# Pairs of token tiles taken from a host-transposed copy of x and normalised by GpSimd, instead of normalised by ScalarE and transposed by TensorE

## The reference

```
x = x + layernorm(attention(layernorm(x)))     # 16 heads of 16, causal softmax, Wq, Wk, Wv, Wo of 256 x 256
x = x + layernorm(moe(layernorm(x)))           # 8 experts, top 2 of a softmax router, 256 -> 2 x 512 -> 256
layernorm(x) = (x - mean(x)) / sqrt(var(x) + 1e-5)     # over the 256 features, no weights
```

## Time and profile before

| | |
|---|---|
| median of 3 runs | 1974.83 us (1972.89 to 1975.65) |
| profiled execution, its own time | 1972.61 us |
| its span, first to last instruction | 1970.9 us |
| TensorE matmul busy | 1843.2 us (94%) |
| VectorE / ScalarE / GpSimd busy | 1541.8 / 1310.9 / 865.1 us |
| mean granted TensorE clock | 0.979 |

### The profile page before, as it was taken

The page is one execution under the profiler, slowest core; times in us unless marked ns, Lnnn a source line. Parts: engine busy times, 40 slices in busy tenths (PEclk is TensorE's granted clock), DMA queues, the critical chain, the costliest instruction groups (busy, mean ns, idle before and its releaser), DMA issues.

```text
span 1970.9 us, 75491 instructions
## 1 busy us (share of the span) xinstructions
PE 1843.2 (94%) x26766; PEld 1280.2 (65%) x26767; DVE 1541.8 (78%) x5221; ACT 1310.9 (67%) x3291; POOL 865.1 (44%) x1247
## 2 busy tenths in 40 slices
PE   6899999999999999999999899999999999999980
PEld 3245555555545555455444369999999999999970
DVE  3888888888888888888888658778777777777767
ACT  5177788888888888888787766554445445554437
POOL 4333343445545555555454744544333333333336
PEclk9799999999999999999999999999999999999995
DMA  7744657475655656465557569889899999998848
GB/s 203 219 120 131 196 171 213 150 208 183 184 172 170 189 154 203 137 192 158 167 163 234 169 206 279 240 250 265 252 260 264 257 264 261 264 262 245 239 119 342
DMA packets 255062, 411.72 MB, mean 209 GB/s; under 512 B 34480, under 2 KB 191920, under 8 KB 247600
## 3 DMA queue, kind: packets, MB, share of 16 engines
q1 hardware_dynamic: 217856, 363.46, 57.7%
q0 software_dynamic: 27120, 35.40, 10.2%
q10 hardware_dynamic: 9792, 8.93, 1.5%
HBM read 284.83 MB, written 122.28 MB: 207 GB/s over the span
## 4 chain that ended last, share of the span: by engine, by line
PE 84%; DVE 6%; ACT 4%; issue 3%; DMA 2%; SPq 1%; POOL 0%; DVEq 0%; ACTq 0%; POOLq 0%
PE ps_s L1544 18%; PE ps_s L1375 12%; PE ps_o L1428 12%; PE ps_e L1375 11%; PE ps_w L1375 11%; PE ps_e L1544 6%; PE ps_e L1561 6%; PE ps_o L1561 6%; DVE cmax L792 2%; ACT space L1275 2%; PE ps_e L1554 1%; ACT arena L1167 1%; DVE space L128 1%; PE ps_w L1504 1%; PE ps_w L1441 1%
## 5 line engine op out<-in xcount | busy, mean ns | idle before, releaser
L1167 ACT ACTIVATE arena<-ps_e 128x512 f32<-128x512 f32 (+3 forms) x1536 | 675.5, 498 | 191.8 <-PE ps_e L1375 179.0
L789 DVE CUSTOM_DVE_ANT_0 arena<-ps_s,c 128x384 bf16<-128x384 f32 (+3 forms) x1024 | 461.7, 485 | 117.2 <-PE ps_s L1375 113.5
L1375 PE MATMUL ps_e<-arena 98*32 98x512 bf16 (+3 forms) x6144 | 505.2, 327 | 28.2 <-ACT arena L1167 27.3
L1375 PE MATMUL ps_s<-arena 96*32 96x512 bf16 (+3 forms) x6144 | 509.0, 333 | 10.7 <-DVE rmax L789 3.7
L792 DVE TENSOR_REDUCE cmax<-ps_s 128x1 f32<-128x512 f32 x512 | 322.5, 680 | 28.9 <-PE ps_s L1375 28.1
L1375 PEld LDWEIGHTS ps_s<-arena 96*32 96x32 bf16 x6144 | 177.8, 96 | 211.7 <-DVE rmax L789 80.8
L1428 PE MATMUL ps_o<-arena 128*32 128x512 f32 (+3 forms) x3072 | 296.3, 486 | 6.1 <-ACT ot L1181 3.2
L1375 PEld LDWEIGHTS ps_e<-arena 98*32 98x32 bf16 x6144 | 177.7, 96 | 178.8 <-issue 82.0
L669 POOL DMA_INDIRECT acc<-blank,place_now x135 | 213.3, 1580 | 140.6 <-POOL place_now L662 66.1
L1544 PE MATMUL ps_s<-arena 128*128 128x128 f32 x2192 | 268.5, 276 | 0.8 <-ACT arena L1314 0.7
L1544 PEld LDWEIGHTS ps_s<-arena 128*128 128x128 f32 x2192 | 261.4, 192 | 8.4 <-issue 3.2
(11 more groups left out here) (182 smaller groups left out, 2714.5 us busy)
## 6 DMA issues: line engine op xcount, KB each, us to landing
arena<-in_gate_up SPq DMA_DIRECT2D x91, 1024.0 KB, 6.0
arena<-qk_parts SPq DMA_DIRECT2D x384, 128.0 KB
c_h<-in_gate_up SPq DMA_DIRECT2D x44, 1024.0 KB
qk_parts<-space SPq DMA_DIRECT2D x120, 192.0 KB, 4.4
d_xin<-xs SPq DMA_DIRECT2D x136, 130.5 KB, 3.4
arena<-v_aug SPq DMA_DIRECT2D x32, 512.0 KB, 5.0
o_t<-ot SPq DMA_DIRECT2D x64, 256.0 KB
v_aug<-space SPq DMA_DIRECT2D x28, 512.0 KB, 5.6
```

The lines of the kernel that those rows point to most:

```text
L789: dve.tensor_tensor_reduce(summed[:, m % RJ, 0:w], ps_s[:, m % RS, 0:w], after[:, HALF - w:HALF], 1.0, LOWEST, ALU.add, ALU.max, rmax[:, p ...
L1167: act.activation(pw[:, at % RP, begin:end], ps_e[:, n % RE, 0:w], ACT.Exp, scale=SCALE).then_inc(e_done, 1)
L1375: last = pe.matmul(out[at:at + QUAD], lhsT[:, at:at + QUAD], rhs, start=start, stop=stop)
```

## The change

For the pairs from 6 to 31 (26 of 32) the host hands in a second copy of x, transposed (`x_turned`, features by tokens). SyncE loads its 256 columns of the pair straight into `xn_t`. TensorE turns the pair's four columns of statistics (1/std and shift of two tiles, `a_norm`, 128 x 4) into four rows by one matmul with the identity; ScalarE copies the 4 x 128 result out; SyncE writes it to memory as four rows of 512 bytes, and loads it back broadcast to all partitions (`norm_rows`, in the place of `xn`). GpSimd then multiplies and adds, two instructions of 128 x 512. The two normalise instructions, the four transposes and the copy to `xn_t` go away for these pairs. The q and k steps of these pairs stand one slot earlier (`Q_AT`); `route` moves from s = 1 to s = 3 of its slot for all pairs. The load of x waits for the statistics alone. Some semaphores are merged, and one 128 x 1 memset of GpSimd goes away. The last fill with ones now waits for `xn_t` of pair 6.

```diff
+    Q_AT = [start if a < FIRST_EVEN else start - 1 for a, start in enumerate(A_AT)]
+    NORM_AT = [start - (12 if a == FIRST_EVEN else 13) for a, start in enumerate(A_AT)]
...
+        norm_rows = space[:, 2560:3072].rearrange("p (z t) -> p z t", z=2)
...
+        turned_v = x_turned.rearrange("(k p) (a t) -> a p k t", p=P, t=WIDE)
+        norms_v = norms.rearrange("a z (c p) -> a (z c) p", p=P)
...
 SyncE
-                        sp.wait_ge(a_xn, a - 1 if a < EARLY else a + 1)
+                        if a < FIRST_EVEN:
+                            sp.wait_ge(a_xn, a - 1 if a < EARLY else a + 1)
+                        else:
+                            sp.wait_ge(a_st, a + 1)
                         sp.dma_start(ax[:, a % 2], x_v[a + 2]).then_inc(ax_in[a % 2], 16)
+                for a in due(A_AT, -12, g):
+                    if a >= FIRST_EVEN:
+                        sp.wait_ge(norms_sb, a - FIRST_EVEN + 1)
+                        sp.dma_start(norms_v[a], norm_row[:]).then_inc(norms_out, 16)
+                for a in due(A_AT, -10, g):
+                    if a >= FIRST_EVEN:
+                        u = a % 2
+                        sp.wait_ge(a_v, a - 1)
+                        sp.wait_ge(a_xt, a)
+                        sp.dma_start(xn_t[:, u], turned_v[a]).then_inc(turned_in, 16)
+                        sp.wait_ge(norms_out, (a - FIRST_EVEN) * 16 + 16)
+                        if a == FIRST_EVEN:
+                            sp.wait_ge(a_tps, FIRST_EVEN)
+                        sp.dma_start(norm_rows, norms[a:a + 1].broadcast_to([P, 2, WIDE])).then_inc(turned_in, 16)
...
 GpSimd
-            pool.memset(pad[:, 0:1], 0.0).then_inc(carried, 1)
-            pool.wait_ge(carried, 1)
...
-                for u, (at, done_by, n) in enumerate(((BEGIN - 2, a_p3, 2 * EARLY + 2), (BEGIN + 6, a_p3, 2 * EARLY + 4), (BEGIN + 9, a_p3, 2 * EARLY + 4))):
+                for u, (at, done_by, n) in enumerate(((BEGIN - 2, a_p3, 2 * EARLY + 2), (BEGIN + 6, a_p3, 2 * EARLY + 4), (BEGIN + 9, a_xt, FIRST_EVEN + 1))):
...
+                for a in due(A_AT, -7, g):
+                    if a >= FIRST_EVEN:
+                        u, mine = a % 2, xn_t[:, a % 2]
+                        pool.wait_ge(turned_in, (a - FIRST_EVEN) * 32 + 32)
+                        pool.tensor_tensor(mine, mine, norm_rows[:, 0:1].broadcast_to([P, KT, WIDE]), ALU.mult).then_inc(a_scaled, 1)
+                        pool.wait_ge(a_scaled, a - FIRST_EVEN + 1)
+                        pool.tensor_tensor(mine, mine, norm_rows[:, 1:2].broadcast_to([P, KT, WIDE]), ALU.add).then_inc(a_xt, 1)
...
-                for a in due(A_AT, 6, g):
+                for a in due(Q_AT, 6, g):
                     third(a, 1)
-                for a in due(A_AT, 3, g):
+                for a in due(Q_AT, 3, g):
                     third(a, 0)
...
 VectorE
-                        for a in due(A_AT, 2, g):
+                        for a in due(Q_AT, 2, g):
                             remainder(a, 0)
-                        for a in due(A_AT, 4, g):
+                        for a in due(Q_AT, 4, g):
                             remainder(a, 1)
...
 ScalarE
                     if s == 1:
+                        for a in due(NORM_AT, 0, g):
+                            if a >= FIRST_EVEN:
+                                act.wait_ge(norms_ps, a - FIRST_EVEN + 1)
+                                if a > FIRST_EVEN:
+                                    act.wait_ge(norms_out, (a - FIRST_EVEN) * 16)
+                                act.activation(norm_row[:], ps_w[0:4, 0:P], ACT.Copy).then_inc(norms_sb, 1)
...
                     if s == 2:
-                        for a in due(A_AT, 0, g):
+                        for a in due(A_AT[0:FIRST_EVEN], 0, g):
                             act.wait_ge(a_tps, a + 1)
...
-                        for a in due(A_AT, 2, g):
+                        for a in due(Q_AT, 2, g):
                             first_part(a, 0)
...
-                        for a in pairs_due(-2, -10, g):
+                        for a in due(A_AT[0:FIRST_EVEN], -2, g):
...
 TensorE
+            def turn_norms(a):
+
+                bank_free()
+                used.append((norms_sb, a - FIRST_EVEN + 1))
+                pe.wait_ge(a_shifted, a + 1)
+                pe.matmul(ps_w[0:4, 0:P], a_norm[:, a % 2].rearrange("p z c -> p (z c)"), consts["ident"],
+                          start=True, stop=True).then_inc(norms_ps, 1)
...
                     if s == 0:
...
+                        for a in due(NORM_AT, 0, g):
+                            if a >= FIRST_EVEN:
+                                turn_norms(a)
-                        for a in due(A_AT, 4, g):
+                        for a in due(Q_AT, 4, g):
                             q_or_k(a, 1, (1,))
                     if s == 1:
-                        for a in due(A_AT, 0, g):
+                        for a in due(A_AT[0:FIRST_EVEN], 0, g):
                             turn_over(a)
-                        for a in due(A_AT, 1, g):
+                        for a in due(Q_AT, 1, g):
                             q_or_k(a, 0, (0, 1))
...
-                        for r in rows_due(16, 17, 17, g):
-                            route(r, 0)
-                            route(r, 1)
...
+                    if s == 3:
                         for r in rows_due(16, 17, 17, g):
                             route(r, 0)
                             route(r, 1)
```

More of the change, by code:

```diff
@@ L153, in combine_stage, with attention_layer @@
     return on_sync, on_gpsimd, on_scalar, on_vector
-def attention_layer(nc, x, wq_t, wk_t, wv_t, wo_t, router_t, router_bias, qk_parts, v_aug, o_t, rden, x1, xs, acc, consts, ident_b, after,
+def attention_layer(nc, x, x_turned, wq_t, wk_t, wv_t, wo_t, router_t, router_bias, qk_parts, v_aug, o_t, rden, norms, x1, xs, acc, consts, ident_b, after,
                     constants_in, kept, expert_weights, w_dn_in, biases_in, gate_up, arena, x1_all, x1_in, load_x1, out):
@@ L271, in attention_layer @@
         a_minus = sb("a_minus", [P, 2, 2])
-        a_rstd = sb("a_rstd", [P, 2, 2])
-        a_shift = sb("a_shift", [P, 2, 2])
+        a_norm = sb("a_norm", [P, 2, 2, 2])
+        a_rstd, a_shift = a_norm[:, :, 0], a_norm[:, :, 1]
+        norm_row = sb("norm_row", [4, P])
         w_o = sb("w_o", [P, KT, D])
@@ L352, in attention_layer @@
         loads, v_loads = ([sem(f"{n}{s}") for s in range(SETS)] for n in ("loads", "v_loads"))
-        rows_in, ones, carried = sem("rows_in"), sem("b_ones"), sem("b_carried")
+        rows_in, ones = sem("rows_in"), sem("b_ones")
         s_scores, s_cmax, s_rmax, s_mhi, s_mlo = (sem("s_" + n) for n in ("scores", "cmax", "rmax", "mhi", "mlo"))
@@ L362, in attention_layer @@
         ax_early = sem("ax_early")
-        a_st, a_agg, a_varred, a_negated, a_rooted, a_shifted = (sem("a_" + n) for n in ("st", "agg", "var", "neg", "root", "shift"))
+        a_st, a_agg, a_moved, a_rooted, a_shifted = (sem("a_" + n) for n in ("st", "agg", "moved", "root", "shift"))
         a_xn, a_tps, a_xt, a_qk, a_p1, a_r1, a_p2, a_p3, a_v, a_vout = (sem("a_" + n) for n in (
@@ L367, in attention_layer @@
         v_out = [sem(f"v_out{u}") for u in range(2)]
+        turned_in, norms_out, a_scaled, norms_ps, norms_sb = (sem(n) for n in ("turned_in", "norms_out", "a_scaled", "norms_ps", "norms_sb"))
         c_weights_in = sem("c_weights_in")
@@ L371, in attention_layer @@
         den_in, rd_out, rd_loads, cx_in = ([sem(f"{n}{u}") for u in range(2)] for n in ("den_in", "rd_out", "rd_loads", "cx_in"))
-        c_den, c_on, c_w, c_raw, c_st, c_agg, c_varred, c_negated, c_rooted, c_shifted = (sem("c_" + n) for n in (
-            "den", "on", "w", "raw", "st", "agg", "var", "neg", "root", "shift"))
+        c_den, c_on, c_w, c_raw, c_st, c_agg, c_moved, c_rooted, c_shifted = (sem("c_" + n) for n in (
+            "den", "on", "w", "raw", "st", "agg", "moved", "root", "shift"))
         c_yn, c_x1, c_hn, c_tps, c_ht, c_r, c_lg, c_top, c_ix = (sem("c_" + n) for n in (
@@ L379, in attention_layer @@
         scattered = [sem(f"scattered{u}") for u in range(2)]
-        base_set, sel_set, zero_at_ready, zeros_out, chain, tables = (sem("g_" + n) for n in ("base_set", "sel_set", "zero_at", "zeros", "chain", "tables"))
+        base_set, zero_at_ready, zeros_out, chain, tables = (sem("g_" + n) for n in ("base_set", "zero_at", "zeros", "chain", "tables"))
         x_in = [sem(f"d_x_in{s}") for s in range(RX)]
@@ L770, in _ @@
             for sel in sels.values():
-                dve.memset(sel[:], 0.0).then_inc(sel_set, 1)
+                dve.memset(sel[:], 0.0).then_inc(base_set, 1)
             for e in range(E):
@@ L1602, in _ @@
                             turn_rows(r)
+                        for n in groups_due(NEVER, 23, g, 1):
+                            rank(n)
+                    if s == 2:
+                        for a in due(Q_AT, 3, g):
```

(7 more changed lines are left out.)

40 lines of the change are left out of this document (19 added, 21 removed).

## The result

The changed kernel takes 2021.82 us (median of 4 runs, 2019.36 to 2025.31) beside 1974.34 us (median of 4, 1972.89 to 1975.65): a ratio of 1.0242, 95% interval 1.0224 to 1.0260. It is 2.4% slower. The profiled execution took 2025.31 us, its span is 2023.6, so that between the two profiled executions there are 52.7 us.

A forecast was written before the change was run, and what follows sets the result against it. TensorE, busy 97%, was taken as the bound. Slots 8 to 0 (+10), slot 7 (+21) and the start (+12) made +43 us on the profiled 1972.6; as a median 2018, less 2 for slack: 2016 us, range 2000 to 2028.

The forecast's parts named there:

- the 2 us taken off for slack: Whole sum: 2018 lowered to 2016 us, since waits that follow each other share slack not visible in one quad.
- The start: Pair 6's loads queue behind SyncE's stores, delaying GpSimd and quad 0's `max_rows`: +12 us, bounds 0 to 16.
- Slots 8 to 0: Transposes and an exponential wait go, new waits come in slots 10 and 0: +0.43 us a quad, 10 us together.
- the old stall: Slot 11, quads 0 to 23: TensorE's wait for an exponential behind `first_part` and the normalise, 1.09 us by starts of matmuls.
- Slot 7: The turning matmul costs 0.24 us and waits for GpSimd's statistics: 1.05 us in 16 quads, 21 us in all.
- The wait for `norm_row`: Slot 7: `route` after s = 3 waits for ScalarE's copy out of the bank, 0.2 us.
- What was covered: GpSimd's 66 us of new work and SyncE's extra issues, some 1.2 us, lie beside other work and cost nothing.
- the sum over quads 4 to 23: Steady quads' new waits: 0.43 us in 20 quads, plus slot 7's 1.05 in 16 and 0.25 in 4.
- Quad 24: It makes the last q and k and had no old stall: +1.5 us.
- The faster rival: The stall doesn't come back in slot 10; each pair gains 1.53 us, 37 us in all: 1938 us, chance 0.08.
- The steady part is even: Only the start costs; slots 7 and 0 wait half as much: 1987 us, chance 0.12.

The follow-up runs named there:

- e1: Changed kernel with pair 6's statistics write and its loads of x and rows issued ahead of the stores of pairs 4 and 5: 2014.36 us, ratio 1.0208.
- e6: Changed kernel with q and k in old slots, statistics turned a slot later, pairs 6 and 7 made the old way: 1962.14 us, ratio 0.9939.
- e2: Changed kernel with only the q and k steps of pairs 6 to 31 back in their old slots: 1994.57 us, ratio 1.0111.
- e8: Changed kernel with the y-normalise of slot 9 covering 8 of its 256 columns: 2020.53 us, ratio 1.0232.
- e3: Changed kernel with GpSimd's four small operations on the statistics ahead of its copy of the maxima rows: 2005.82 us, ratio 1.0162.
- e4: Changed kernel with GpSimd's two products per pair on 8 columns in place of 512, all waits kept: 2021.66 us, ratio 1.0255.
- e5: Changed kernel with q and k in old slots, statistics turned in slot 8, and `route` back after s = 1 of slot 7: 1970.36 us, ratio 0.9987.
- e7: e6 with the first step of `q_or_k(a, 1)` moved from s = 2 to s = 3 of slot 11: 1965.77 us, ratio 0.9959.

## Why the prediction was right

The forecast was 2016 us; the median is 2021.8, 2.4% slower, where 2.1% was said. The range held it, and the mechanism was right in all three parts. The sum as it was added up was 2018; the 2 us taken off for slack rest on no row.

**The start: right.** Said: loads in at 90, GpSimd at `mpart` at 96, `max_rows` at 96.7, a net 12 us. Measured: 89.25, 95.50, 95.89 and 12.55 us at quad 0. e1 shows the cause (the queue) and e6 that nothing else of it remains: its first `max_rows` starts at 81.84. That 12.55 lies so near to 12 is in part luck. The forecast went from 14 to 12 by the transposes and by what leaves ScalarE; the clock, which it left out, moved that same step by about 1 us, as far as three runs can tell (-1.0, -0.5 and +0.1 with 7.6, 9.4 and 12.1 us at half clock).

**Slots 8 to 0: right in sum and in parts.** Said: the old stall gone, 1.10 us in slot 10, 1.10 in slot 0 (0.65 and 0.45), +0.43 a quad. Measured in the quad shown: 626.95 - 625.91 = 1.04 and 1.13, and in the same quad slots 8 to 0 together take 0.45 us longer. e2 removed those waits with the slots, and e8 took 0.42 us off the one of slot 10 with the instruction that I had named.

**Slot 7: right.** Said 1.05 us; slot 7 is 1.14 longer in the quad shown, and quads 0 to 3 grow by 3.0 in sum (0.79 to 0.84 in three of them, 0.59 in the fourth) where 3.6 was said. The matmul itself costs 0.27 in the quads with `rank`, where it waits for nothing; 0.24 was said. The wait for `norm_row` is there too: `route` starts at 618.82, 0.14 after the copy ends (618.43 + 0.25). e3 shows the place of the wait: 0.8 of it went with GpSimd's order.

**What was covered: right, but for one row.** e4 shows that GpSimd's 66 us (931.6 busy after, 865.1 before; the forecast's own 26 x 2.6 is 67.6) cost the plain quads nothing. SyncE's extra issues left no engine waiting for a load between 100 and 1100 us beyond what there was before. VectorE's two `hot` operations did take longer beside the new products, by 0.57 us and not by 1.3 to 2.5, and that cost TensorE 0.27 us a time, not up to 2.5 (last section). The forecast said that the trace of before had no such pair of operations to read this from. It had one, in VectorE's order of time: an operation with two SBUF inputs that takes 0.17 us elsewhere lasted 0.62, until 1130.30, beside a GpSimd cut of 0.64 us that ended at 1130.26.

```profile
1129.68 0.62 DVE L869 TENSOR_TENSOR c_h<-ex,rtotal 128x8 f32<-128x8 f32 x1
```

**The mis-sized term** is the sum over quads 4 to 23: 26.4 us were said (20 x 0.43 = 8.6, 16 x 1.05 = 16.8 and 4 x 0.25 = 1), 31.4 measured. A plain quad is right to a tenth (1.48 said, 1.57 measured), which is 1.4 us in 16 quads. Four quads with `hot` add 4 x 0.27. Quads 4 and 5 are below the pattern (0.97 and 0.67), by 1.5 together, and those with `rank` below what was said, by 0.5. Quads 8 and 14 add 0.9 and 0.5, which e1, with the same steady part, does not show; I take them for this one execution's. The largest part, 2.9 us, came in quad 19, in which the turning matmul waited 1.95 us instead of 0.66. GpSimd and TensorE in order of time there:

```profile
793.63 0.79 POOL L716 DMA_DIRECT2D arena<-mrow  x1 [2.87 <-issue]
```

```profile
796.02 0.27 PE L1481 MATMUL ps_w<-c,a_norm 128*4 128x128 f32 x1 [1.95 <-POOL a_norm L729]
```

GpSimd's copy of the maxima rows began 1.58 us after they were ready instead of 0.3, with nothing in the profile that it waited for. The kernel before has the same, in GpSimd's order of time:

```profile
756.69 0.79 POOL L695 DMA_DIRECT2D arena<-mrow  x1 [2.86 <-issue]
```

This is no accident of one execution. All ten traces have it, at this one copy of the 32, behind 60 other DMAs of GpSimd: it begins 1.58 us after the rows are ready in nine of them and 1.74 in e3; only e1 has a second one, at 88.90. So it hangs on the place in the program; what it is stays open. In the kernel before nobody waited for what stood behind it, and it cost nothing, nor did it in e5, e6 and e7, where the statistics are turned later. In e1 and e4 slots 6 and 7 of that quad take 1.3 us more for it. In the changed kernel they take 2.7 more, because TensorE's clock then fell to half for 3.4 us, right after the wait; in e1 and e4 the same wait came and the clock stayed full, in e2 and e8 it fell too:

```profile
796.34:799.75 3.41, 3.41 (x61) 1.74 (x56) 2.40 (x6) 1.94 (x4) 1.86 (x3) 0.50 0.22 79
```

The forecast had no term for either. Quad 24 took 1.2 where 1.5 was said. Last, 2.96 us in quad 28, behind the last changed pair, and 2.0 after quad 30 stand in no term. The first can be followed. A load of `den` that SyncE issued at 1095.94 took 9.6 us to land, where 2.2 is the median of such transfers around it, so VectorE's reciprocal came late, and the operation behind it fell on a product of GpSimd that it misses otherwise. VectorE and GpSimd in order of time:

```profile
1105.61 0.36 DVE L1053 RECIPROCAL den<-den 128x32 f32<-128x32 f32 x1 [0.66 <-DMA den<-o_t]
1107.57 1.27 DVE L855 CAST at_f<-top_at 128x16 f32<-128x16 uint32 x1
```

```profile
1107.55 1.25 POOL L761 TENSOR_TENSOR x_sb<-c_y,c_x 128x512 f32<-128x512 f32 x1
```

That cast takes 0.17 us otherwise. TensorE waited up to 1.3 us for the maxima behind it, and its clock was at half from 1110.37 to 1113.78. e1 has all of this (2.97 us); e7 has the late load and the long cast but the full clock (1.9 us); e2 to e6 have neither, the cast takes 0.17, and the quad grows by 0.13 or less. Why the load was slow stays open. The 2.0 us after quad 30 lie within what this part differs by among the traces (-1.0 to 2.3).

**The faster rival, and what it missed.** It would have had each pair gain 1.53 us, 1938 in all. e5 and e6 give TensorE all that this rival asked for: no wait for an exponential in slots 8 to 0, and a turning matmul that hardly waits. They gain 0.82 a pair. Slot 8 gives 0.50 (0.44 asked), but slot 11 gives 0.32 instead of 1.09: the other 0.77 is what `remainder` and the maxima hold there once the exponential's wait is gone (0.69 in e2). In the changed kernel `remainder` stands a slot earlier, and the whole 1.09 was gone, so that my own forecast did not need this number; the expectation of e2 failed on it, and that of e7 took the chain for shorter than it is.

**A rival that was priced wrong.** "The steady part is even" was to hold if slots 7 and 0 waited half as much. By the forecast's own terms that takes off about 0.5 in 20 quads for each, some 20 us of 31, and would give near 1997 and not 1987. Neither wait was smaller, so nothing came of it.

## What to carry to other kernels

When an engine's work is cut in order to remove a wait, look for the second chain that ends just behind the one removed: here 0.3 to 0.4 us of a stall of 1.09 could be had, and moving the other work up a slot to fill the gap cost more than that. A small step that feeds the busiest engine must stand ahead of the DMA issues and waits of its own engine and be asked for a slot after it is ready, not in the slot in which it is made: that alone was 0.8 us a quad here. And the first use of a new transfer is a case of its own: what it stands behind in the queue at the start of a stage cost a quarter of the whole loss, and leaving the first two pairs as they were got it back. Last, a change of order can make operations of other engines meet that did not meet before, far from the change: look for instructions that last longer than others of their kind.

## What the runs showed of the hardware

**VectorE and GpSimd exclude each other, by the row.** In slot 1 of the changed kernel VectorE's `hot` operation (128 x 64, both inputs in SBUF) falls on GpSimd's first product, in VectorE's and GpSimd's order of time:

```profile
420.99 0.79 DVE L861 TENSOR_TENSOR hot<-c,at_f 128x64 f32<-128x64 f32 x1
```

```profile
420.41 1.28 POOL L734 TENSOR_TENSOR space<-space 128x512 f32<-128x512 f32 x1
```

Before, the same operation took 0.22 us (535.28). Now it lasts 0.79, until 421.78, and the product ended at 421.69: it did nothing until GpSimd was done. In e4, where the products last 0.20 us, it met the next long GpSimd operation instead (`third`, 562.57 to 563.74) and took 1.16. The cost on TensorE follows the length of the block: pairs of `hot` operations that take 0.92, 1.10 and 1.29 us (0.36 alone) go with quads whose growth is above that of plain ones by 0.27 (changed kernel and e3), 0.45 (e2, e5, e6) and 0.6 (e4). The Trainium skill (SBUF — State Buffer, Who interferes with whom) says that a VectorE instruction with two SBUF inputs contends with a GpSimd one that reads SBUF, by an exclusive lock; these rows agree.

Two inputs are not needed for it. The cast of quad 28 reads one, and lasted 1.27 us instead of 0.17, until 1108.84; GpSimd's product beside it ended at 1108.80. In e8 the same cast falls beside a cut of GpSimd in quads 8, 12, 16, 20 and 24 as well (0.61 us each, and slot 10 some 0.34 longer), and a `TENSOR_SCALAR` of 128 x 8 took 1.92 us instead of 0.16. No edit touched these operations; what differed is when VectorE and GpSimd came to them.

**A narrow ScalarE instruction is not cheap.** The y-normalise on 128 x 8 took 0.39 us (median, e8) and on 128 x 256 0.60; the copy of 4 x 128 took 0.25. What a narrower operation saves has to be read from such a row and not scaled by columns.
